# One values transfer in two pieces, and a later place for two quotients

## The chip, the cores and the metric

The kernel runs on one NeuronCore of a Trainium2 chip. The metric is the device time of one launch in microseconds. TensorE is PE (its weight loads PEld), VectorE is DVE, ScalarE is ACT, GpSimd is POOL; SyncE (SP) issues every transfer of the stages told here.

## The reference

A decoder layer over 16 batches of 112 tokens, 1024 wide, in float32, with a layer norm behind each of three parts:

```
s = silu(x @ Wg.T); in each row the half of s with the smallest |s| is set to 0
x = norm(x + (s * (x @ Wu.T)) @ Wd.T)                   # inner width 2752
q = x @ Wq (32 heads of 32); k, v = ctx @ Wk, ctx @ Wv  # 375 context rows, 8 key-value heads
x = norm(x + softmax(q k / sqrt(32)) v @ Wo)            # 4 query heads share a key-value head
x = norm(x + bf16(x) @ dequantized 4-bit weights)
```

## The kernel before

There are four passes. `context_pass` projects the context to keys and values and stores them in DRAM. `gated_query_pass` does the gated part and the queries, and stores the queries. `attend_pass` (L1292) does the attention of one batch after another, and `finish_pass` (L1660) the output projection and the last part. Each pass is a block: each engine runs its own instruction list, engines wait for each other by semaphores, and a block ends when all engines have ended theirs.

To keep float32 accuracy at a fast matmul rate, an operand is split into a high part (a rounded copy) and a low part (the rest).

In `attend_pass` a batch n has 24 steps x, three for each of the 8 key-value heads h; a step is one third (125 rows) of the 375 context rows. PE's list for a step: the transposed scores of that third (`scores`, L1616), one third of the product of the values with the exponentials of the head three heads earlier (`values`, L1635; L1629 for head 3, which isn't split), and in 16 of 24 steps a pair of score products for the next batch (`first_pair`, L1601) from which DVE takes row maxima (`maxima`, L1530). At step 18 PE turns the maxima (L1607), at step 19 ACT makes their high part (L1473), at step 20 DVE the low part (L1534), and SP writes both into the operand of the next batch (`put_max`, L149).

ACT takes the exponential of the scores (L1483), makes the high part of heads 1, 2, 4 (L1490) and copies each head's product out of PSUM (`take`, L1497); before it takes a head's product it waits, at even heads, until the store of an earlier one has landed. DVE makes the high part of heads 0, 5, 6, 7 (L1544). POOL makes all low parts (L1463) apart from head 3's; in the first eight batches it also makes one low part of the output weights each (L1451). In the last batch DVE makes the low parts of heads 2, 5 and 7 itself (`split_lo`, L1562). The buffers for the high and the low parts are three deep each.

SP's list for a batch: stacks of keys and queries for the next two batches in quarters (`fetch_qk`, four transfers each, L145), stores of the products of two heads (`put_o`, L1398 and L1400), a load of output weights in the first eight batches (L1411), and at head 7 the values of the next batch: `fetch_v`, L1387, one transfer (L1390) of 125 rows (partitions) of 6336 bytes from DRAM into one of two buffers, once the product of the batch before has been read. PE waits for the values at the first product of a batch, which is at step 9 of that batch. The values of batch 0 are loaded in the pass before (L841), at its step 26.

In the last batch SP also loads the numerators, addends and reciprocals of the first two tiles of `finish_pass` (`load_tile`, L169). `quotients(i)` (L1552) on DVE waits for those of tile i, adds (L1555) and multiplies (L1557). It stands in DVE's list at step 14 (tile 0) and at step 17 (tile 1) of the last batch. DVE's high and low parts of head h come at step 3(h + 1), those of head 7 behind the last step. ACT then makes the high part of tile 0 behind its last exponential (L1519) and POOL its low part behind its last low part of the attention (L1466). `finish_pass` starts with the high and low part of tile 1, PE with 8 idle products and the projection of tile 0.

Of the kernel before, what the change touches and what calls it, by code (L numbers as in the profile page):

```python
# [6 lines left out]
F32 = mybir.dt.float32  # L7
# [9 lines left out]
B, S, D = 16, 112, 1024  # L17
# [13 lines left out]
KN = C // KT  # L31
# [37 lines left out]
class Carry:  # L69
# [67 lines left out]
    def fetch_qk(self, sp, qd, kd, n, f):  # L137

        p, stack = n % 2, 3 * HD
        q_rows = self.qs[p][:, f].bitcast(F32).rearrange("d j m q -> d (j m q)")  # L140
        k_rows = self.ks[p][:, f].bitcast(F32).rearrange("d v c -> d (v c)")
        key = kd[n, 2 * (f % 2) + f // 2]
        for dst, src in ((q_rows[0:2 * HD], qd[n, f]), (k_rows[0:HD], key[0:HD]),
                         (q_rows[2 * HD:stack], qd[n, f, 0:HD]), (k_rows[HD:stack], key)):
            sp.dma_start(dst, src).then_inc(self.qk_loaded[p][f], 16)  # L145

    def put_max(self, eng, n, i):

# [477 lines left out]
def gated_query_pass(nc, cy, x_t, w_gu, w_d, w_d_tail, x_tok, w_q, ident_f, ident_b, y_dram, y1_dram, qd, q_v, k_v, vd):  # L626
# [28 lines left out]
    with ExitStack() as ctx:  # L655
# [95 lines left out]
        def _(sp):  # L751
# [61 lines left out]
            for n in range(XR, NALL + AHEAD + 4):  # L813
                if n < NALL:
                    load(n)
                g, c = divmod(n, N_CH)
                if c == DOWN + CC + 7 and g < G:
                    store_y(g, 0)
                if g > 0 and c == 7:
                    store_y(g - 1, 1)  # L820
                if g + 1 < G and c + 2 in X_AT:
                    load_x(g + 1, X_AT.index(c + 2))
                p = n - N - AHEAD
                for b in tokens_at(p + 2):
                    load_y(b)
                    load_tokens(b)
                for b in turn_at(p - 1):
                    store_y1(b)
                if 0 <= p - 3 < G * KD:
                    store_q(p - 3)  # L830
                if p == 20:
                    cy.await_context(sp)
                    for s in q_stored:
                        sp.wait_ge(s, 32 * KD // NQO)
                    for f in range(2):
                        cy.fetch_qk(sp, q_v, k_v, 0, f)
                if p == 23:
                    for f in range(2, NQK):
                        cy.fetch_qk(sp, q_v, k_v, 0, f)
                if p == 26:  # L840
                    sp.dma_start(cy.vs0[:].bitcast(F32).rearrange("p t v w -> p (t v w)"), vd[0]).then_inc(cy.v_loaded[0], 16)  # L841
                if p == 28:
                    for i in range(XS):
                        sp.wait_ge(y1_stored[i], 16 * len(range(i, B, XS)))
                    sp.wait_ge(back, 2 * B)
                    for f in range(2):
                        cy.fetch_qk(sp, q_v, k_v, 1, f)
                if p == 32:
                    sp.wait_ge(cy.nmh, 1)
                    cy.put_max(sp, 0, 0)  # L850
                    sp.wait_ge(cy.nml, 1)
                    cy.put_max(sp, 0, 1)
# [439 lines left out]
def attend_pass(nc, cy, kd, vd, qd, w_o, wo_hi, wo_lo, ident_f, od, rd):  # L1292
# [11 lines left out]
    PAIR_OF = {x: y for y, x in enumerate(PAIR_AT)}  # L1304
    TURN_AT = 18
    RECIP_AT = 22
    QUOTIENTS_AT = (14, 17)
    FULL = (3,)
    HI_ACT = (1, 2, 4)
    HI_DVE = tuple(h for h in range(KV) if h not in HI_ACT + FULL)  # L1310
# [11 lines left out]
    with ExitStack() as ctx:  # L1322
# [4 lines left out]
        vs = [cy.vs0, m.sb("vs1", [KN, KT, KV, VW], F32R)]  # L1327
# [12 lines left out]
        (t_scored, exped, hi_act, hi_dve, lo_pool, lo_dve, pv, o_taken, wo_hi_done, wo_lo_done) = (m.sem(n) for n in names)  # L1340
        ones, scored, maxed, nm_turned, nmh, nml, nm_put = (cy.ones, cy.scored, cy.maxed, cy.nm_turned, cy.nmh, cy.nml,
                                                            cy.nm_put)
        qk_loaded, v_loaded, o_put, recip, r_stored = cy.qk_loaded, cy.v_loaded, cy.o_put, cy.recip, cy.r_stored
        wo_loaded = [m.sem(f"wo_loaded{i}") for i in range(2)]
        block = ctx.enter_context(nc.Block())
        QK = 4 * 16
# [33 lines left out]
        @block.sync  # L1380
        def _(sp):
            def fetch_qk(n, f):
                if n >= 2:
                    sp.wait_ge(t_scored, NX * (n - 2) + NX // NQK * (f + 1))
                cy.fetch_qk(sp, qd, kd, n, f)

            def fetch_v(n):  # L1387
                if n >= 2:
                    sp.wait_ge(pv, KV * (n - 1))
                sp.dma_start(vs[n % 2][:].bitcast(F32).rearrange("p t v w -> p (t v w)"),  # L1390
                             vd[n]).then_inc(v_loaded[n % 2], 16)

            def put_o(u):

                n, h = divmod(2 * u, KV)
                row = n % GB * H + h * REP
                sp.wait_ge(o_taken, 2 * u + 2)
                sp.dma_start(od[n, h:h + 2].rearrange("h s d j q -> (s d) h (j q)"),  # L1398
                             o_ab[u % NO][0:2 * HD]).then_inc(o_put[u % NO], 16)
                sp.dma_start(den[n // GB % 2][row:row + 2 * REP, :],  # L1400
                             o_ab[u % NO][2 * HD:2 * HD + 1].rearrange("p h (j q) -> p (h j) q", q=S)
                             ).then_inc(o_put[u % NO], 16)

            def put_recip(c):
                sp.wait_ge(recip, c + 1)
                cy.put_recip(sp, rd, c)

            def load_w(k):
                if k >= 2:
                    sp.wait_ge(wo_lo_done, k - 1)  # L1410
                sp.dma_start(wo_raw[k % 2][:], w_o[:, k, :]).then_inc(wo_loaded[k % 2], 16)  # L1411

            fetch_qk(1, NQK - 2)
            cy.await_queries(sp)
            for n in range(B):
                for h in range(KV):
                    if h == 0 and n + 1 < B:
                        fetch_qk(n + 1, NQK - 1)
                    if h in (2, 4) and n + 2 < B:
                        fetch_qk(n + 2, h // 2 - 1)  # L1420
                    if h == TURN_AT // KT and n + 1 < B:
                        sp.wait_ge(nmh, n + 2)
                        cy.put_max(sp, n + 1, 0)
                        sp.wait_ge(nml, n + 2)
                        cy.put_max(sp, n + 1, 1)
                        if n + 2 < B:
                            fetch_qk(n + 2, NQK - 2)
                    if h == W_LOAD_AT and n < KV:
                        load_w(n)
                    if h == V_AT and n + 1 < B:  # L1430
                        fetch_v(n + 1)
                    if h == 2 and n == B - 1:
                        sp.wait_ge(t_scored, NX * n)
                        sp.wait_ge(r_stored, 16 * (B - GB))
                        for i in range(2):
                            load_tile(sp, od, rd, i, cy.num[i], cy.add[i], cy.rec[i], cy.o_loaded[i])
                    if (KV * n + h - LAG) % 2 == 0 and KV * n + h - LAG >= 2:
                        put_o((KV * n + h - LAG) // 2 - 1)
                    if h == RECIP_AT // KT and n % GB == 0 and n > 0:
                        put_recip(n // GB - 1)  # L1440
            for u in range((KV * B - 1 - LAG) // 2, KV * B // 2):
                put_o(u)
# [81 lines left out]
        def _(dve):  # L1524
# [27 lines left out]
            def quotients(i):  # L1552

                dve.wait_ge(cy.o_loaded[i], 16 * tile_loads(i))
                nc.vector.tensor_tensor(cy.num[i][:], cy.num[i][:], cy.add[i][:], ALU.add)  # L1555
                dve.drain()
                nc.vector.tensor_tensor(cy.num[i][:], cy.num[i][:], cy.rec[i][:], ALU.mult).then_inc(cy.normed, 1)  # L1557
# [7 lines left out]
            def follow(g):  # L1565
                if g % KV in HI_DVE:
                    split_hi(g)
                if by_dve(g):
                    split_lo(g)
# [4 lines left out]
            for n in range(B):  # L1574
                for x in range(NX):
                    h, t = divmod(x, KT)
                    for pair in pairs_at(n, x):
                        maxima(*pair)
                    if t == 0 and KV * n + h >= 1:
                        follow(KV * n + h - 1)  # L1580
                    if x == RECIP_AT and n % GB == 0 and n > 0:
                        invert(n // GB - 1)
                    if x == TURN_AT + 2 and n + 1 < B:
                        max_lo(n + 1)
                    if n == B - 1 and x in QUOTIENTS_AT:
                        quotients(QUOTIENTS_AT.index(x))
            follow(KV * B - 1)

        @block.tensor
        def _(pe):  # L1590
# [28 lines left out]
            def values(g, i):  # L1619

                n, h = divmod(g, KV)
                if i == 0:
                    if h == 0:
                        pe.wait_ge(v_loaded[n % 2], 16 * (n // 2 + 1))
                    if g >= 2:
                        pe.wait_ge(o_taken, g - 1)
                    await_hi(pe, g)
# [337 lines left out]
```

## Time and profile before

| | |
|---|---|
| median of 3 runs | 2531.68 us (2531.49 to 2536.49) |
| the profiled execution | 2542.13 us, span 2540.3 us |
| mean granted clock of PE | 0.98 |
| attention stage | about 1855 to 2308 us of the span |

Times in the rows are microseconds from the start of the span. PE is the engine with the most work. A matmul's end is modelled, so its idle time before the next can read 0.3 to 0.4 us less than the idle time of the weight loads (PEld) at the same place. The idle time before an instruction and what ended it stand in square brackets. The granted clock is a share of 2.4 GHz; 0.50 is 1.2 GHz.

### The profile page before, as it was taken

How to read it: one execution, taken by the hardware profiler on the slowest of the kernel's cores; microseconds unless marked ns; L12 is line 12 of the kernel's file. 1: busy time of each engine (PE TensorE's matmuls, PEld its weight loads, DVE VectorE, ACT ScalarE, POOL GpSimd, SP SyncE). 2: the span in 40 equal slices, each digit the busy share in tenths (PEclk: the TensorE clock that was granted, in tenths of full speed). 3: DMA queues.
4: the chain of work that ended last, by engine and by line, in shares of the span. 5: the costliest groups of instructions: out<-in, count | busy, mean ns of one | idle time of the engine just before them, and what ended most of it. 6: DMA issues, size and time to landing. Idle time of an engine off the chain costs nothing. (4 is left out here: it accounts for less than half of the span.)

```text
span 2540.3 us, 33218 instructions
## 1 busy us (share of the span) xinstructions
PE 2435.3 (96%) x12861; PEld 2126.1 (84%) x12874; DVE 1268.1 (50%) x1779; ACT 1049.1 (41%) x1531; POOL 1402.1 (55%) x626
## 2 busy tenths in 40 slices
PE   9999999999999999999999999999988888888998
PEld 9999999988999889999899998899866666656775
DVE  4762304861018820079400486254467777764665
ACT  2112235533337333363423553233266767681111
POOL 5344244865447755458554585454467887782221
PEclk9999999999999999999999999999998999998999
DMA  6565533333332343333333233589956765555772
GB/s 206 169 189 176 195 112 100 106 117 125 113 100 100 123 127 113 100 101 126 108 115 115 96 108 98 186 256 292 264 150 160 188 168 150 154 151 158 177 175 87
DMA packets 254447, 371.75 MB, mean 146 GB/s; under 512 B 126641, under 2 KB 178865, under 8 KB 254033
## 3 DMA queue, kind: packets, MB, share of 16 engines
q1 hardware_dynamic: 254288, 369.61, 49.0%
q8 instruction: 103, 1.69, 0.3%
q14 instruction: 56, 0.45, 0.1%
HBM read 290.15 MB, written 78.70 MB: 145 GB/s over the span
## 5 line engine op out<-in xcount | busy, mean ns | idle before, releaser
L995 POOL TENSOR_TENSOR gp_w_lo<-cy_raw,gp_w_hi 128x1024 fp32r<-128x1024 f32 (+2 forms) x299 | 721.0, 2413 | 611.8 <-ACT gp_w_hi L870 611.3
L183 PE MATMUL gp_acc<-gp_x_hi,gp_w_hi 128*128 128x448 f32 x1504 | 558.6, 371 | 2.6 <-ACT gp_row L921 2.5
L185 PE MATMUL gp_acc<-gp_x_hi,gp_w_lo 128*128 128x448 f32 x1504 | 550.2, 366 | 0.0
L184 PE MATMUL gp_acc<-gp_x_lo,gp_w_hi 128*128 128x448 f32 x1504 | 550.1, 366 | 0.0
L870 ACT CAST gp_w_hi<-cy_raw 128x1024 fp32r<-128x1024 f32 (+2 forms) x300 | 307.1, 1026 | 315.0 <-PE gp_acc L185 308.7
L1463 POOL TENSOR_TENSOR ap_e_lo<-ap_e,ap_e_hi 125x1344 fp32r<-125x1344 f32 x109 | 331.0, 3069 | 95.4 <-ACT ap_e_hi L1490 74.7
L183 PEld LDWEIGHTS gp_acc<-gp_x_hi,gp_w_hi 128*128 128x128 f32 x1504 | 283.2, 188 | 25.9 <-ACT gp_row L921 4.0
L185 PEld LDWEIGHTS gp_acc<-gp_x_hi,gp_w_lo 128*128 128x128 f32 x1504 | 282.9, 188 | 22.1
L184 PEld LDWEIGHTS gp_acc<-gp_x_lo,gp_w_hi 128*128 128x128 f32 x1504 | 283.3, 188 | 20.9
L481 DVE TENSOR_REDUCE gp_sel_unit<-gp_keys 112x4 f32<-112x2048 f32 x4 | 9.1, 2286 | 550.3 <-ACT gp_keys L882 550.3
L183 PE MATMUL gp_acc<-gp_h_hi,gp_w_hi 128*128 128x448 f32 (+1 forms) x704 | 267.9, 381 | 8.4 <-DVE gp_h_lo L1058 5.6
L1530 DVE TENSOR_REDUCE cy_n_max<-ap_p_s 112x2 f32<-112x750 f32 x240 | 221.5, 936 | 80.7 <-PE ap_p_s L1601 78.6
L184 PE MATMUL gp_acc<-gp_h_lo,gp_w_hi 128*128 128x448 f32 (+1 forms) x704 | 259.4, 368 | 0.0
L185 PE MATMUL gp_acc<-gp_h_hi,gp_w_lo 128*128 128x448 f32 (+1 forms) x704 | 259.3, 368 | 0.0
L1483 ACT ACTIVATE ap_e<-ap_p_t 125x448 f32<-125x448 f32 x384 | 204.6, 543 | 120.5 <-PE ap_p_t L1616 116.1
L330 POOL TENSOR_TENSOR cp_c_lo<-cp_c_raw,cp_c_hi 128x1504 fp32r<-128x1504 f32 x32 | 110.7, 3479 | 145.0 <-ACT cp_c_hi L299 145.0
L474 DVE TENSOR_SCALAR_CACHE_REDUCE gp_keep<-gp_keys,gp_sel_bound 112x2752 bf16<-112x2752 f32 (+1 forms) x56 | 158.2, 2867 | 63.9 <-ACT gp_keys L882 61.6
L1616 PE MATMUL ap_p_t<-cy_qs,cy_ks 98*125 98x448 f32 x384 | 161.5, 422 | 2.7 <-DMA cy_qs<-cy_nm_lo 1.9
L888 ACT ACTIVATE gp_act<-gp_acc 128x448 f32<-128x448 f32 x84 | 45.7, 544 | 274.4 <-PE gp_acc L185 274.4
L183 PEld LDWEIGHTS gp_acc<-gp_h_hi,gp_w_hi 128*128 128x128 f32 (+1 forms) x704 | 133.7, 190 | 23.6 <-DVE gp_h_lo L1058 6.8
L185 PEld LDWEIGHTS gp_acc<-gp_h_hi,gp_w_lo 128*128 128x128 f32 (+1 forms) x704 | 133.4, 189 | 11.6
L184 PEld LDWEIGHTS gp_acc<-gp_h_lo,gp_w_hi 128*128 128x128 f32 (+1 forms) x704 | 133.8, 190 | 9.9
(207 smaller groups left out, 4355.1 us busy)
## 6 DMA issues: line engine op xcount, KB each, us to landing
cy_raw<-in_w_gu SPq DMA_DIRECT2D x172, 512.0 KB, 3.3
cy_raw<-in_w_d SPq DMA_DIRECT2D x80, 512.0 KB, 3.6
cp_c_raw<-in_ctx_t SPq DMA_DIRECT2D x32, 750.0 KB, 6.7
cy_raw<-in_w_q SPq DMA_DIRECT2D x32, 512.0 KB, 4.6
q_scratch<-gp_q_out SPq DMA_DIRECT2D x64, 224.0 KB, 6.2
cy_qs<-q_scratch SPq DMA_DIRECT2D x64, 224.0 KB, 4.1
k_scratch<-cp_k_out SPq DMA_DIRECT2D x32, 376.0 KB
cy_ks<-k_scratch SPq DMA_DIRECT2D x64, 188.0 KB, 4.8
```

The source lines that it names most:

```text
L183: nc.tensor.matmul(out, wh, xh, start=first, stop=False)
L184: nc.tensor.matmul(out, wh, xl, start=False, stop=False)
L185: return nc.tensor.matmul(out, wl, xh, start=False, stop=last)
L330: nc.gpsimd.tensor_tensor(c_lo[p][:, ks(h), :], c_raw[p][:, ks(h), :], c_hi[p][:, ks(h), :].bitcast(F32), ALU.subtract).then_inc(lo_done, 1)
L474: self.nc.vector.tensor_scalar(self.keep[:, b, 0:width], self.keys[:, b, 0:width], bound[:, b:b + 1], None, op, ALU.add, accum_out=self.co ...
L870: last = nc.scalar.copy(o, i)
L888: nc.scalar.activation(act_t[:, c, :], a[:, 0:T], ACT.Silu).then_inc(evac, 1)
L995: last = nc.gpsimd.tensor_tensor(o, i, hi.bitcast(F32), ALU.subtract)
L1463: nc.gpsimd.tensor_tensor(e_lo[g % NLO][:], e[g % NE][:], e_hi[g % NHI][:].bitcast(F32), ALU.subtract).then_inc(lo_pool, 1)
L1483: nc.scalar.activation(e[g % NE][:, x % KT, :], p_t[x % 2][0:KN, 0:T], ACT.Exp, scale=SCALE).then_inc(exped, 1)
L1530: nc.vector.reduce_max(n_max[:, h // 2, 2 * a:2 * a + 2, h % 2], p_s[y % 2][:, :, 0:C], AX_X).then_inc(maxed, 1)
L1616: nc.tensor.matmul(p_t[x % 2][0:KN, 0:T], ks[p][0:KR, h // 2, h % 2, t * KN:(t + 1) * KN], qs[p][:, h // 2, :, h % 2, :], start=True, stop ...
```

## The change

A new method `Carry.fetch_v` issues two transfers for the values of a batch, rows 0 to 111 and rows 112 to 124, both on the same semaphore, so that the waiting value is 32 a batch in place of 16. Both places that load values call it. In the last batch of `attend_pass` the quotients of tile 0 move from step 14 to step 18, behind DVE's high and low part of head 5, and those of tile 1 from step 17 to the end of DVE's list, behind the high and low part of head 7.

```diff
+    def fetch_v(self, sp, vs, vd, n):
+
+        flat = vs[:].bitcast(F32).rearrange("p t v w -> p (t v w)")
+        for rows in (slice(0, S), slice(S, KN)):
+            sp.dma_start(flat[rows], vd[n, rows]).then_inc(self.v_loaded[n % 2], 16)
...
                 if p == 26:
-                    sp.dma_start(cy.vs0[:].bitcast(F32).rearrange("p t v w -> p (t v w)"), vd[0]).then_inc(cy.v_loaded[0], 16)
+                    cy.fetch_v(sp, cy.vs0, vd, 0)
...
-    QUOTIENTS_AT = (14, 17)
+    QUOTIENTS_AT = 18
...
             def fetch_v(n):
                 if n >= 2:
                     sp.wait_ge(pv, KV * (n - 1))
-                sp.dma_start(vs[n % 2][:].bitcast(F32).rearrange("p t v w -> p (t v w)"),
-                             vd[n]).then_inc(v_loaded[n % 2], 16)
+                cy.fetch_v(sp, vs[n % 2], vd, n)
...
-                    if n == B - 1 and x in QUOTIENTS_AT:
-                        quotients(QUOTIENTS_AT.index(x))
+                    if n == B - 1 and x == QUOTIENTS_AT:
+                        quotients(0)
             follow(KV * B - 1)
+            quotients(1)
...
-                        pe.wait_ge(v_loaded[n % 2], 16 * (n // 2 + 1))
+                        pe.wait_ge(cy.v_loaded[n % 2], 32 * (n // 2 + 1))
```

## Rows read from the trace of the kernel before

**Rows 1.** The page, busy time, share of the span and count of each engine.
```profile
PE 2435.3 (96%) x12861; PEld 2126.1 (84%) x12874; DVE 1268.1 (50%) x1779; ACT 1049.1 (41%) x1531; POOL 1402.1 (55%) x626
```

**Rows 2.** Waits from 1850 to 2300: engine, line, releaser: total us, times, longest.
```profile
PEld ap_p_o L1635 <- POOL ap_e_lo L1463: 23.8, 19, 2.3
PEld ap_p_o L1635 <- DMA cy_vs<-v_scratch: 20.1, 7, 4.5
PEld ap_p_o L1635 <- DMA ap_vs<-v_scratch: 17.9, 7, 4.2
PEld ap_p_s L1601 <- DVE cy_n_max L1530: 10.4, 10, 1.8
```

**Rows 3.** Stretches between issues of the values: length, busy times, PE clock, DMA share, GB/s.
```profile
1880.41:2104.34 223.93, 192.56 (x840) 138.43 (x839) 169.77 (x202) 158.92 (x295) 189.20 (x65) 0.93 0.65 171
2104.34:2241.93 137.59, 118.46 (x529) 85.79 (x527) 105.42 (x128) 98.26 (x181) 106.34 (x36) 0.94 0.61 157
2241.93:2266.10 24.17, 21.47 (x95) 15.50 (x94) 18.50 (x23) 17.85 (x33) 18.96 (x7) 0.93 0.42 115
```

**Rows 4.** The same view, columns PE, PEld, DVE, ACT, POOL: two single batches.
```profile
1996.32:2021.11 24.79, 22.41 (x107) 16.06 (x106) 21.73 (x27) 19.74 (x38) 23.73 (x9) 1.00 0.74 197
2129.37:2159.55 30.18, 24.47 (x104) 17.64 (x103) 21.33 (x27) 19.41 (x36) 21.73 (x8) 0.89 0.57 145
```

**Rows 5.** PE's timeline: start, us, line, tiles; one pair of products a step.
```profile
2144.47 0.83 PE L1601 MATMUL ap_p_s<-cy_ks,cy_qs 96*112 96x376 f32 x2
2146.22 0.83 PE L1601 MATMUL ap_p_s<-cy_ks,cy_qs 96*112 96x376 f32 x2
2147.68 0.51 PE L1601 MATMUL ap_p_s<-cy_ks,cy_qs 96*112 96x376 f32 x2
2148.63 0.51 PE L1601 MATMUL ap_p_s<-cy_ks,cy_qs 96*112 96x376 f32 x2
```

**Rows 6.** Timeline: two issues of the values on SP, and PE's first use of each.
```profile
1996.32 0.48 SPq L1390 DMA_DIRECT2D ap_vs<-v_scratch  x1
2006.47 0.20 PEld L1635 LDWEIGHTS ap_p_o<-ap_e_hi,ap_vs 125*66 125x66 f32 x2 [0.79 <-DMA ap_vs<-v_scratch]
2129.37 0.48 SPq L1390 DMA_DIRECT2D cy_vs<-v_scratch  x1
2141.92 1.01 PE L1635 MATMUL ap_p_o<-ap_e_hi,cy_vs 125*66 125x448 f32 x2 [4.15 <-DMA cy_vs<-v_scratch]
```

**Rows 7.** Stretches of 1 us; the values issued at 2159.55 let PE go at 2171.52.
```profile
2168.00:2169.00 1.00, 0.00 (x0) 0.00 (x0) 0.00 (x0) 1.00 (x2) 1.00 (x1) 1.00 1.00 241
2172.00:2173.00 1.00, 1.00 (x5) 0.93 (x4) 0.00 (x0) 0.00 (x0) 1.00 (x1) 0.50 0.33 97
```

**Rows 8.** The page, DMA issues: count, KB each, median us to landing.
```profile
cp_c_raw<-in_ctx_t SPq DMA_DIRECT2D x32, 750.0 KB, 6.7
ap_wo_raw<-in_w_o SPq DMA_DIRECT2D x8, 512.0 KB, 10.1
```

**Rows 9.** Timeline of the last batch's end, all engines.
```profile
2283.62 0.98 ACT L1483 ACTIVATE ap_e<-ap_p_t 125x448 f32<-125x448 f32 x2
2291.93 1.23 DVE L1555 TENSOR_TENSOR cy_num<-cy_num,cy_add 128x1024 f32<-128x1024 f32 x1 [3.56 <-DMA cy_rec<-r_scratch]
2292.78 0.53 ACT L1497 COPY ap_o_ab<-ap_p_o 66x448 f32<-66x448 f32 x1 [2.92 <-DMA cy_den<-ap_o_ab]
2294.37 1.55 DVE L1544 TENSOR_SCALAR_CACHE_REDUCE ap_e_hi<-ap_e 125x1344 fp32r<-125x1344 f32 x1
2296.07 1.35 PE L1635 MATMUL ap_p_o<-ap_e_hi,ap_vs 125*66 125x448 f32 x3 [7.55 <-DVE ap_e_hi L1544]
2300.74 2.78 DVE L1562 TENSOR_TENSOR ap_e_lo<-ap_e,ap_e_hi 125x1344 fp32r<-125x1344 f32 x1
2307.01 0.68 SPq L1400 DMA_DIRECT2D cy_den<-cy_o_ab  x1
2308.43 0.10 POOL L1739 MEMSET fp_neg_half<- 128x1 f32 x1 [2.69 <-POOLq L1322]
```

More of the change, by code:

```diff
@@ L1342, in attend_pass @@
                                                             cy.nm_put)
-        qk_loaded, v_loaded, o_put, recip, r_stored = cy.qk_loaded, cy.v_loaded, cy.o_put, cy.recip, cy.r_stored
+        qk_loaded, o_put, recip, r_stored = cy.qk_loaded, cy.o_put, cy.recip, cy.r_stored
         wo_loaded = [m.sem(f"wo_loaded{i}") for i in range(2)]
```

## The prediction

> **What bounds the kernel now.** I read the page's busy shares first, then the waits of the attention stage, then that stage by stretches, and last single instructions. PE is busy in 96% of the span [rows 1]; most of the kernel is a PE stream, and only holes in it can be won. Of the weight loads' waits in the attention stage (about 1855 to 2308 us), the longest by cause are those of the value products for the values transfer: 20.1 + 17.9 = 38.0 us in 14 times, one for each batch from the second to the fifteenth. Behind them come POOL's low parts (23.8 us) and DVE's maxima (10.4 us) [rows 2]. The 0.1 us by which such a wait overstates the loss is left in.
>
> The stretches are cut at the issues of the values transfer: eight of them in 223.93 us, five in 137.59, the last in 24.17; clocks 0.93, 0.94, 0.93 [rows 3]. The two stretches of rows 4 show what a wait costs: 24.79 us at clock 1.00 where PE waited 0.79, 30.18 us at 0.89 where it waited some 4.5. So a long wait is paid twice. Behind it PE runs at half clock (1.2 of 2.4 GHz) for a few microseconds: one step of the loop takes 1.75 us (2144.47 to 2146.22), a step at full clock 0.95 [rows 5].
>
> The transfer is slow. Issued at 2129.37, it let PE go at 2141.92, 12.55 us later; the quickest took 10.15 us (1996.32 to 2006.47) [rows 6]. The mean of the fourteen is 11.7. PE would have been ready 8.2 us after the issue (2137.6; its wait is read from the same row) and 9.4 us after it in the other. Why slow: early in the transfer all DMA engines are busy (share 1.00, 241 GB/s), but at its end and just behind it the share stays at 0.33 with 97 GB/s [rows 7]. That is 5 engines of 16 (0.31). Five engines carry its 125 rows, and what was queued behind it on those five still runs while eleven rest.
>
> **The split of the transfer.** It now goes as 112 rows and 13 rows. What does it take? From below: on five engines each carries 773.4 / 5 = 155 KB in 11.7 us; 693 KB on sixteen is 43 KB each, at the same pace 3.3 us, with the second issue (0.48 us later, the issue's own length in rows 6) 3.8 us. From above: the 512 KB rows of the output weights, 128 partitions wide and in this same stage, land after 10.1 us [rows 8]; by size that is 15.3 us for 773.4 KB, and it is the far end. The nearest row in size and width is the context's 750 KB in 6.7 us [rows 8]: 6.9 us by size, 7.4 with the second issue. I take 7.4. The weights' row is the worse guide, because it is issued behind four stacks of keys and queries and its own share of the five clogged engines comes last. 7.4 is under the 8.2 to 9.4 us that PE leaves, with only 0.8 us to spare in the tightest.
>
> What goes, by groups of stretches. Waits: 19.5 us in the eight, 16.2 in the five, 2.25 in the last (together the 38.0 of rows 2). Half clock: at most (1 - clock) x length, 15.7, 8.3 and 1.7 us [rows 3]; part of that time passed in waiting, and some dips may have another cause, so I take three quarters: 11.8, 6.2, 1.3. New lengths:
> - the eight: 223.93 - 19.5 - 11.8 = 192.6 us. POOL is the next limit: it worked 189.20 us in them [rows 3], seven low parts a batch and the weights' in addition. They can't be shorter than 189.2. In the 24.79 us stretch POOL was busy 23.73 us [rows 4], so this limit has been touched already.
> - the five: 137.59 - 16.2 - 6.2 = 115.2 us; POOL's work there is 106.34, DVE's 105.42 [rows 3], both below.
> - the last: 24.17 - 2.25 - 1.3 = 20.6 us, over POOL's 18.96.
> Sum 328.4 against 385.69: 57.3 us less. What is late next is then POOL's low part in the first half, and in the second DVE's maxima by a little.
>
> The extra issue costs SP 0.48 us in each of 15 batches. Behind it in SP's queue stand two output transfers and the last quarter of the next keys and queries, needed some 15 steps later; they now find no clogged engines. The row maxima are issued ahead of it. I cost it at nothing; without that cover it is 0.48 x 15 = 7 us. The transfer for the first batch, issued in the stage before, has tens of microseconds.
>
> **The closing batch.** DVE makes the next pass's quotients before head 5's high part and waits for their data: until 2291.93, 3.56 us; the high part comes only at 2294.37, PE waits 7.55 us for it until 2296.07 [rows 9]. Now head 5's scores, exponentiated at about 2284.1 (first of the pair at 2283.62), are split at once. Step by step, with a high part of DVE at 1.55 us, a pass of quotients at 1.23 and a low part at 2.78 where POOL works beside it [rows 9], without POOL like a high part, 1.6: high 5 to 2285.8, low 5 to 2287.4, first quotients (two passes and a gap) to 2289.9, high 6 to 2291.5, high 7 to 2293.1, low 7 to 2295.9. POOL's low 6 runs from 2291.5 to 2294.6 (106.34 us for some 35 of them in rows 3, 3.0 each). PE: head 5 by 2290.5; head 6 not before ACT has taken head 4's outputs, which waits for a store and ended at 2293.31 [rows 9], so 2293.3 to 2295.9; head 7 to 2298.2 at half clock. ACT takes it by 2298.8, SP's last two stores are issued by 2300.2 (before: 0.59 + 0.67 us, the last at 2307.01), and the next pass opens 0.7 us behind: 2300.9 against 2308.43 [rows 9], 7.5 us less. DVE's second quotients, now last, end near 2299.6 to 2300.9 if POOL slows them and lie beside this. Bounds: nothing, if the end of the pass waits for them and for their data; 9.4 us, if all of PE's waits go. The pass behind is PE-bound and moves forward whole.
>
> **Sum.** 57.3 + 7.5 = 64.8 us. The profiled execution took 2542.13 us (span 2540.3), 10.4 above the median of 2531.68. 2542.13 - 64.8 = 2477.3; by the ratio of the two, 2467 us.
>
> **Rivals.**
> 1. The next limits bite earlier. The waits gave POOL and DVE time to catch up; that goes. For it: POOL already holds PE 23.8 us. Against: rows 4, where 24.79 us passed with hardly a wait. Price: the eight at 24.8 us (198.3), the five at 24.2 (121), the last 22.2, the closing batch 5: 44 + 5 = 49 us less, 2483.
> 2. The transfer is hidden only in part. It lands near 10.2 us, today's quickest, because DMA is busy on all engines when it starts [rows 7]. PE then waits 1 to 2 us a batch, 17 to 20 us, without the dips: about 46 us less, 2486.
> 3. The split brings nothing: the bytes, not the engines, set the pace. 241 GB/s at full share speaks for it, the 0.33 at the end against. Only the closing batch remains, less up to 7 us of issues: 2531.7 - 7.5 + 7 = 2531. (The Trainium skill, page "DMA: Bandwidth & Descriptors", section "Rules for kernel authors": two transfers to disjoint partitions are not worth it, since both use the same engines; use one 128-partition transfer. It presupposes halves that each spread over all 16, and the share of 0.33 in rows 7 says that the one transfer of today doesn't. By the rule the time would be this rival's 2531, by the row the forecast.)
> 4. Slower. The values on all 16 engines queue behind the keys and queries everywhere, as the output weights do, and land after 15.3 us. Each of 14 waits grows by 15.3 - 11.7 = 3.6 us: 50 us, less 7.5: 2574. It decides once the mean landing is over 11.7 + 7.5 / 14 = 12.2 us. For it stands the 10.1 of rows 8; against it, that no transfer would then find idle engines, and eleven are idle in rows 7.
>
> **How the numbers follow.** Forecast 0.64, rivals 0.14, 0.12, 0.06 and 0.04. The forecast's own range is 2456 to 2476: all of the half-clock losses and 9.4 us at one end (the eight at POOL's 189.2: 34.7 + 24.5 + 4.0 + 9.4 = 72.6 us, 2459), a closing batch without gain at the other (57.3 us, 2475), and 1 to 3 us on each side for the runs' own spread. With the first two rivals the range is 2456 to 2492. About 0.2%, 5 us, can be told from no change. Faster: the forecast and rivals 1 and 2, 0.9 and a little; same: rival 3; slower: rival 4.
>
> **What the profile would show.** Right: no wait of the value products for values in the waits of the attention stage, or under 3 us in all; clocks of 0.98 and more by stretch; stretches of about 24.1 us in the first half and 23.0 in the second; the DMA share no longer lingering at 0.33; the wait of 7.55 us gone, and one of 2 to 3 us for ACT's taking of head 4 in its place. Wrong: waits for the values that remain at 1 us and more (rival 2), more than 35 us of waits for POOL and over 20 for DVE's maxima (rival 1), or row maxima that arrive later, which would put the extra issue or the fuller engines on the path.

## The result and the profile after

The changed kernel takes 2477.14 us (2475.1 to 2481.15, 4 runs) against 2533.91 us (4 runs) of the kernel before: ratio 0.9778, 95% interval 0.976 to 0.9796. The forecast was 2467 us with a range of 2456 to 2492. Run again twice, the changed kernel had ratios of 0.9776 and 0.9767. By the medians the gain is 56.8 us, and 64.7 were forecast; the time lies 1 us outside the forecast's own range (2456 to 2476), in the part that the range has by rivals 1 and 2.

The profiled execution took 2481.15 us (span 2479.3), 61.0 us under the one of before; the forecast's sum was 64.8. Where the 61.0 us came from, cut at the first and last issue of the values transfer and at the opening of the next pass, as in [rows 3, 9]:

| part | before | after | less | forecast |
|---|---|---|---|---|
| up to the first such issue of the attention | 1880.41 | 1877.33 | 3.1 | 0 |
| first eight stretches | 223.93 | 198.89 | 25.0 | 31.3 |
| next five | 137.59 | 116.26 | 21.3 | 22.4 |
| last | 24.17 | 20.58 | 3.6 | 3.6 |
| from the last issue to the next pass | 42.33 | 34.66 | 7.7 | 7.5 |
| the next pass | 231.87 | 231.58 | 0.3 | 0 |

The first row is no part of the change: in the kernels told below this moment lay between 1870.7 and 1879.9 us, whatever was changed behind it.

The waits of the attention stage after, 1850 to 2260 us (engine, line, releaser: total us, times, longest):
```profile
PEld ap_p_o L1641 <- POOL ap_e_lo L1468: 33.8, 37, 2.3
PEld ap_p_s L1607 <- DVE cy_n_max L1535: 11.2, 10, 1.8
PEld ap_p_o L1641 <- ACT ap_o_ab L1502: 4.5, 8, 3.0
PEld ap_p_o L1641 <- DMA cy_vs<-v_scratch: 0.8, 1, 0.8
PE ap_p_o L1641 <- POOL ap_e_lo L1468: 18.2, 12, 1.9
```
Of 38.0 us of waits for the values in 14 times one of 0.8 us is left [rows 2]. The weight loads' waits for POOL have grown from 23.8 to 33.8 us, and from 19 to 37 times. The last line is PE's own idle time for the same cause, and that has hardly grown. Before, the view had:
```profile
PE ap_p_o L1635 <- DMA cy_vs<-v_scratch: 17.7, 7, 4.2
PE ap_p_o L1635 <- POOL ap_e_lo L1463: 16.2, 11, 1.9
PE ap_p_o L1635 <- DMA ap_vs<-v_scratch: 15.6, 7, 3.8
```
So the two engine rows of one wait differ: 38.0 us by the weight loads is 33.3 us by PE.

The stretches after (ends, length, busy PE, PEld, DVE, ACT, POOL, clock, DMA share, GB/s), first by group, then four single batches of the first eight and one of the five:
```profile
1877.33:2076.22 198.89, 183.89 (x840) 129.66 (x839) 169.53 (x202) 157.61 (x295) 189.85 (x65) 0.98 0.71 192
2076.22:2192.48 116.26, 111.01 (x529) 81.10 (x527) 105.27 (x128) 97.12 (x181) 106.75 (x36) 1.00 0.69 186
2192.48:2213.06 20.58, 19.74 (x95) 14.35 (x94) 18.49 (x23) 17.52 (x33) 19.04 (x7) 1.00 0.51 136
...
1902.02:1926.68 24.66, 22.77 (x107) 15.88 (x106) 21.11 (x26) 19.78 (x38) 23.71 (x9) 1.00 0.71 196
1926.68:1952.08 25.40, 23.51 (x107) 17.33 (x106) 21.12 (x26) 19.94 (x38) 23.76 (x9) 0.93 0.70 191
1952.08:1976.78 24.70, 22.80 (x107) 15.88 (x106) 21.13 (x26) 19.77 (x38) 23.73 (x9) 1.00 0.75 196
2001.44:2026.88 25.44, 23.53 (x105) 17.09 (x104) 21.14 (x26) 19.73 (x37) 23.72 (x9) 0.93 0.70 192
2122.61:2145.46 22.85, 21.99 (x107) 16.20 (x106) 20.77 (x26) 19.32 (x37) 21.30 (x8) 1.00 0.71 189
```
The clock is 1.00 where it was 0.94 [rows 3], apart from two batches of the first eight at 0.93, which are 0.75 us longer than their neighbours. The DMA share rose from 0.65 and 0.61 to 0.71 and 0.69: the same bytes in less time. It no longer lingers near 5/16: of the slices of 1 us between the first and the last issue of the values, 48 of 385 had a share of 0.30 to 0.36 before, and 9 of 335 have it now.

One batch's waits of PE for POOL after, from PEld's timeline:
```profile
1906.94 0.13 PEld L1641 LDWEIGHTS ap_p_o<-ap_e_lo,ap_vs 125*66 125x66 f32 x1 [2.26 <-POOL ap_e_lo L1468]
1909.97 0.13 PEld L1641 LDWEIGHTS ap_p_o<-ap_e_lo,ap_vs 125*66 125x66 f32 x1 [0.37 <-POOL ap_e_lo L1468]
1913.01 0.13 PEld L1641 LDWEIGHTS ap_p_o<-ap_e_lo,cy_vs 125*66 125x66 f32 x1 [0.49 <-POOL ap_e_lo L1468]
1916.06 0.13 PEld L1641 LDWEIGHTS ap_p_o<-ap_e_lo,cy_vs 125*66 125x66 f32 x1 [0.38 <-POOL ap_e_lo L1468]
1919.11 0.14 PEld L1641 LDWEIGHTS ap_p_o<-ap_e_lo,cy_vs 125*66 125x66 f32 x1 [0.39 <-POOL ap_e_lo L1468]
```
After the wait of 2.3 us PE walks at POOL's pace, one head in 3.05 us, for four heads more. Before, such a row held the first wait and the 0.36; then the values' wait came and POOL had caught up.

The end of the last batch after, answering to [rows 9]:
```profile
2238.95 0.96 ACT L1502 COPY ap_o_ab<-ap_p_o 66x448 f32<-66x448 f32 x2 [1.08 <-DMA cy_den<-ap_o_ab]
2239.53 0.72 PE L1641 MATMUL ap_p_o<-ap_e_hi,ap_vs 125*66 125x448 f32 x2 [2.60 <-ACT ap_o_ab L1502]
2241.35 3.68 POOL L1471 TENSOR_TENSOR cy_o_lo<-cy_num,cy_o_hi 128x1024 fp32r<-128x1024 f32 x1
2241.44 1.38 PE L1641 MATMUL ap_p_o<-ap_e_lo,ap_vs 125*66 125x448 f32 x3 [0.81 <-POOL ap_e_lo L1468]
2242.72 3.38 DVE L1560 TENSOR_TENSOR cy_num<-cy_num,cy_add 128x1024 f32<-128x1024 f32 x1
2246.18 1.23 DVE L1562 TENSOR_TENSOR cy_num<-cy_num,cy_rec 128x1024 f32<-128x1024 f32 x1
2246.30 0.67 SPq L1405 DMA_DIRECT2D cy_den<-cy_o_ab  x1
2247.72 0.10 POOL L1745 MEMSET fp_neg_half<- 128x1 f32 x1 [2.69 <-POOLq L1328]
```
The wait of 7.55 us for DVE is gone; 2.60 us for ACT's taking of head 4 stands in its place, as forecast. DVE's last quotients end at 2247.41, 0.44 us behind SP's last store (issue over at 2246.97). The next pass opens 0.75 us behind that issue, as it did before (0.74 us, where DVE had nothing late); so the store explains the opening, and the quotients end beside it. The trace doesn't show which of the two is the last.

### The profile page after: what moved, and what is told of

Read it like the earlier page. It is cut to its first block and busy times, and to the rows that moved or that the text cites. A ratio compares the mean times of both kernels' runs of the same rounds, so it can differ in the third digit from the quotient of the medians.

```text
span 2479.3 us, 33234 instructions
## 1 busy us (share of the span) xinstructions
PE 2412.9 (97%) x12861; PEld 2108.1 (85%) x12874; DVE 1269.1 (51%) x1779; ACT 1046.4 (42%) x1531; POOL 1403.4 (57%) x626
## 5 line engine op out<-in xcount | busy, mean ns | idle before, releaser
L1468 POOL TENSOR_TENSOR ap_e_lo<-ap_e,ap_e_hi 125x1344 fp32r<-125x1344 f32 x109 | 332.1, 3083 | 36.6 <-ACT ap_e_hi L1495 23.8
L189 PEld LDWEIGHTS gp_acc<-gp_h_hi,gp_w_hi 128*128 128x128 f32 (+1 forms) x704 | 133.1, 189 | 23.5 <-DVE gp_h_lo L1064 6.8
L191 PEld LDWEIGHTS gp_acc<-gp_h_hi,gp_w_lo 128*128 128x128 f32 (+1 forms) x704 | 132.9, 189 | 11.8
```

The lines of the kernel that those rows point to most:

```text
L189: nc.tensor.matmul(out, wh, xh, start=first, stop=False)
L191: return nc.tensor.matmul(out, wl, xh, start=False, stop=last)
L1468: nc.gpsimd.tensor_tensor(e_lo[g % NLO][:], e[g % NE][:], e_hi[g % NHI][:].bitcast(F32), ALU.subtract).then_inc(lo_pool, 1)
```

## The experiments

### The split alone

```diff
-    QUOTIENTS_AT = 18            # changed kernel
+    QUOTIENTS_AT = (14, 17)      # and both quotients back there
```


> The changed kernel with the quotients back at steps 14 and 17. Theory (two independent gains): the stretches between the issues of the values are as in the changed kernel, 198.9 + 116.3 + 20.6 us (together 335.7 against 385.7 before), and the end of the last batch is as before, from the last issue of the values to the next pass 42.3 us against 34.7 in the changed kernel. Time about 53 us under the kernel before, ratio 0.979 to 0.980. Rival (the closing batch only looked faster because it started without a backlog): the end takes under 38 us even with the quotients at their old steps, and the time equals the changed kernel's.

Measured: 2487.79 us, ratio 0.9789 (0.9764 to 0.9814). The stretches:
```profile
1879.85:2081.53 201.68, 186.42 (x839) 133.94 (x838) 169.59 (x202) 157.77 (x295) 189.80 (x65) 0.96 0.69 189
2081.53:2197.27 115.74, 111.03 (x529) 81.34 (x528) 105.28 (x128) 97.10 (x181) 106.74 (x36) 1.00 0.69 187
2197.27:2217.94 20.67, 19.85 (x95) 14.33 (x94) 18.51 (x23) 17.60 (x33) 19.02 (x7) 1.00 0.49 134
```
Together 338.1 us against 385.7 of before, and 41.5 us from the last issue to the next pass. The stretches' gain belongs to the split alone, the end's to the quotients. The stretches show this and the ratios don't: the intervals of this kernel and of the changed one overlap. The rival falls, since the end took 41.5 us and not under 38. The 2.4 us over the forecast 335.7 are half-clock dips: five batches of the first eight ran 25.4 us or longer at a clock of 0.93 here, two in the changed kernel's first profile.

### The quotients alone

```diff
-    QUOTIENTS_AT = (14, 17)      # kernel before
+    QUOTIENTS_AT = 18            # and quotients(1) behind follow(KV * B - 1)
```


> The kernel before with the quotients at step 18 and at the end of DVE's list; values in one transfer of 125 rows. Theory: 7.7 us less, all behind the last issue of the values (34.7 us from there to the next pass instead of 42.3), ratio about 0.997; the fourteen waits for the values stay at 38 us. Rival: the end is limited by something that the split brought, and the ratio is 1.000.

Measured: 2525.55 us, ratio 0.9952 (0.9934 to 0.9969). The end took 34.6 us, and the waits for the values were still 34.7 us:
```profile
PEld ap_p_o L1636 <- POOL ap_e_lo L1463: 23.5, 15, 2.3
PEld ap_p_o L1636 <- DMA cy_vs<-v_scratch: 18.4, 7, 3.9
PEld ap_p_o L1636 <- DMA ap_vs<-v_scratch: 16.3, 8, 4.3
```
The ratio says 12 us, the place of the change 7.7; the interval's upper end, 0.9969, is 7.9 us. The stretches were 6 us shorter than before without a reason in the edit (one profiled execution each), so the end's length is the better measure.

### The cut at row 115

```diff
-        for rows in (slice(0, S), slice(S, KN)):
+        for rows in (slice(0, 115), slice(115, KN)):
```


> The changed kernel with the values cut at row 115 in place of row 112: again two transfers with nearly the same sizes, but 115 = 5 x 23. Theory (what matters is over how many DMA engines the long piece goes, 5 here as for 125 rows): each of the five engines has 23 rows in place of 25, so that the landing takes about 11 us and the waits for the values come back, 28 to 36 us in all, with half clock behind them; the DMA share lingers at 0.33; ratio to the kernel before 0.985 to 0.995. Rival (two pieces in flight, or a smaller first one, are what helps): as the changed kernel, ratio 0.978, hardly a wait for values.

Measured: 2528.05 us, ratio 0.9941 (0.9912 to 0.997). Waits and stretches:
```profile
PEld ap_p_o L1641 <- DMA cy_vs<-v_scratch: 20.6, 7, 4.4
PEld ap_p_o L1641 <- DMA ap_vs<-v_scratch: 17.5, 7, 5.3
```
```profile
1879.29:2103.48 224.19, 194.01 (x840) 140.60 (x839) 169.54 (x202) 159.65 (x295) 189.28 (x65) 0.92 0.66 170
2103.48:2244.36 140.88, 120.38 (x529) 87.13 (x528) 105.47 (x128) 98.42 (x181) 106.31 (x36) 0.93 0.60 154
```
Two signs of the five engines are back as well: a DMA share of 0.32 (the last number but one of the first line) in the slice at whose end one batch's values landed, issued at 2160.34, and the output weights' landing, here and then in the changed kernel (DMA issues from 1850 to 2300: count, KB, median us to landing):
```profile
2172.00:2173.00 1.00, 0.00 (x0) 0.00 (x0) 0.00 (x0) 0.00 (x0) 1.00 (x1) 0.50 0.32 92
ap_wo_raw<-in_w_o SPq DMA_DIRECT2D x8, 512.0 KB, 9.9
ap_wo_raw<-in_w_o SPq DMA_DIRECT2D x8, 512.0 KB, 5.4
```
All of the split's gain is gone: 38.1 us of waits and clocks of 0.92 and 0.93, as before. Over the 13 waits ahead of the last batch the values landed 12.0 us behind their issue (before, over its 14: 11.7). Two pieces bring nothing by themselves, nor does a first piece shorter by 8%; three rows decide. 125 and 115 both divide by 5, and both leave a share near 5/16; 112 divides by 16 and leaves hardly any. The output weights land after 10.1 us with 125 rows [rows 8], 9.9 with 115 and 5.4 with 112: it was the values' five engines that held them up. I had expected somewhat shorter waits (28 to 36 us). The Trainium skill, "DMA: Bandwidth & Descriptors", section "Why a DMA increments its semaphore by 16 and not by 1", says that a transfer uses the largest number of engines up to 16 that divides its slowest dimension. By that rule it is 16 for 112 rows, 5 for 125 and for 115. The traces agree: a DMA share of 0.33 behind the 125 rows [rows 7], of 0.32 behind the 115, and 115 rows as slow as 125.

### The values issued late

```diff
                     if h == 0 and n + 1 < B:
                         fetch_qk(n + 1, NQK - 1)
+                    if h == 0 and n > 0:
+                        fetch_v(n)
-                    if h == V_AT and n + 1 < B:
-                        fetch_v(n + 1)
```


> The changed kernel with the values' issue moved behind the last quarter of the keys and queries, about 4 us later, so that PE waits for them in every batch and the time from issue to landing can be read. It settles the 7.4 us of the prediction, which the changed kernel's trace can't show where nothing waits. Expected: landing 6.5 to 8.5 us behind the issue (forecast 7.4), so waits of 2 to 4 us in each of 15 batches and a time some 40 us over the changed kernel's. If the landing is over 9 us, the changed kernel is hidden only by an earlier issue's luck; at 4 us, the pace per engine of the old transfer (13 KB a us) was the better guide than the context's 6.7 us.

Measured: 2517.85 us (one run). PE waited for the values in 12 batches, 31.0 us. The longest and the shortest landing:
```profile
2148.28 1.02 SPq L151 DMA_DIRECT2D ap_vs<-v_scratch  x2
2157.09 0.30 PEld L1641 LDWEIGHTS ap_p_o<-ap_e_hi,ap_vs 125*66 125x66 f32 x2 [5.41 <-DMA ap_vs<-v_scratch]
...
2207.79 1.02 SPq L151 DMA_DIRECT2D ap_vs<-v_scratch  x2
2213.32 0.30 PEld L1641 LDWEIGHTS ap_p_o<-ap_e_hi,ap_vs 125*66 125x66 f32 x2 [3.59 <-DMA ap_vs<-v_scratch]
```
8.81 and 5.53 us; the mean of the 12 is 7.1 us, where 6.5 to 8.5 had been expected, and the waits were 0.5 to 5.4 us in 12 batches, not 2 to 4 in 15. The batches without a wait can't be read; they landed in time. The forecast's 7.4 holds as a mean, and the spread explains the changed kernel's one wait: its values landed 8.84 us behind their issue (2145.46 to 2154.30), and PE was ready after 8.0.

### Four pieces

```diff
-        for rows in (slice(0, S), slice(S, KN)):
+        for rows in (slice(0, 48), slice(48, 96), slice(96, S), slice(S, KN)):
```


> The changed kernel with the values in four transfers (48, 48, 16 and 13 rows), each but the last over 16 engines. It prices the extra issue that the prediction put at nothing: SP gets two more, some 1 us a batch. Theory (SP has room and nothing behind it in its queue is late): stretches within 0.2 us a batch of the changed kernel's, ratio 0.978, waits for the values under 3 us in all. Rival (an issue of 0.5 us goes to the path): 15 to 16 us more, ratio 0.984. The landing of the last piece moves by 1 us, so a few waits of under 1 us may appear.

Measured: 2479.24 us, ratio 0.977 (0.9744 to 0.9797). Stretches 200.70, 115.66 and 20.59 us, end 34.65, and no wait for the values at all. SP's issues take 1.95 us a batch in place of 1.02. The rival's 15 us aren't there: the first eight are 1.8 us longer than the changed kernel's 198.89, with four batches at a clock of 0.93 where that had two, and the other stretches aren't longer. The extra issues cost nothing that can be seen.

### The weights' low part at head 4

```diff
-    W_LOAD_AT, W_SPLIT_AT = 3, 6
+    W_LOAD_AT, W_SPLIT_AT = 3, 4
...
-                    if x == KT * W_SPLIT_AT + 2 and n < KV:
+                    if x == KT * W_SPLIT_AT - 1 and n < KV:
```
(SP loads the weights one batch earlier, those of batch 0 at its start.)

> The changed kernel with the output weights' low part on POOL ahead of head 4's low part instead of behind head 5's, ACT's high part of them at step 11 instead of 20, and their load a batch earlier. It looks at why the first eight stretches took 198.9 us and not the 192.6 forecast. Theory (the place of that piece of work: it stands in the middle of POOL's unbroken row, PE waits 2.3 us for the next low part in each of eight batches, while POOL idles 0.8 us at head 4 of the next one): the stretches fall from 24.7 to about 23.9 us, PE's waits for POOL from 33.8 us to under 20, 5 to 7 us less than the changed kernel, ratio 0.9755. Rival (POOL's total work of 23.7 us a batch sets the pace, wherever the piece stands): the stretches stay at 24.7 and the waits only move to another head.

Measured: 2467.98 us, ratio 0.9717 (0.9689 to 0.9744). The first eight stretches as one, and the waits for POOL:
```profile
1876.29:2067.02 190.73, 185.02 (x840) 125.41 (x839) 167.35 (x202) 158.39 (x295) 188.83 (x65) 1.00 0.72 197
```
```profile
PEld ap_p_o L1643 <- POOL ap_e_lo L1470: 31.9, 59, 1.4
```
PE's own idle time for POOL within the first eight stretches, in the changed kernel and here:
```profile
PE ap_p_o L1641 <- POOL ap_e_lo L1468: 14.5, 8, 1.9
PE ap_p_o L1643 <- POOL ap_e_lo L1470: 4.6, 16, 0.3
```
The stretches of the first half fall to 23.9 us (the first 23.5), 8 us less in all, with no dip of the clock. POOL is busy for 188.83 of 190.73 us, 99%: now its amount is the limit; in the changed kernel it was the order of the work (POOL busy for 95%). The edit moved three things, POOL's piece, ACT's high part and the load, and no run parts them. The weight loads' waits for POOL hardly fell in sum (31.9 us; I had expected under 20), and I had read that sum as lost time. It isn't: PE's own idle time fell by 9.9 us, and the stretches by 8.2. The wait of 2.3 us a batch is gone, and the small waits of the weight loads that stand in its place mostly pass while PE still multiplies. In a second profile of the changed kernel that sum is 27.9 us, less than the 33.8 of the first, though its first eight stretches are 3.6 us longer.

Again, beside the changed kernel, five runs of each:

> The changed kernel, as the measure for the next one on the same chip: ratio 0.978, first eight stretches 199 to 203 us by the number of half-clock dips behind the 2.3 us waits for POOL.

> The kernel with the weights' low part at head 4 once more, now beside the changed kernel on one chip. Theory (place, not amount, of POOL's work): first eight stretches 190.7 us at clock 1.00 with no wait for POOL over 1.4 us, 8 to 12 us less than the changed kernel, ratio 0.973 or lower, and the two intervals apart. Rival (the first run of it was a lucky chip): ratio within 0.002 of the changed kernel's.

Changed kernel 2480.47 us (2477.73 to 2482.93), ratio 0.9767 (0.9742 to 0.9791); this one 2470.13 us (2467.69 to 2472.59), ratio 0.9732 (0.9708 to 0.9756). First eight stretches 198.85 and 190.80 us. The intervals of the ratios overlap by 0.0014, against what was expected; the runs themselves, five each, don't overlap, and the difference is 10.3 us. This version beats both kernels.

### The end reordered

```diff
-    QUOTIENTS_AT = 18
+    QUOTIENTS_AT = 21
...
+                    if h == 5 and n == B - 1:       # tile 1's load, out of h == 2
+                        load_tile(sp, od, rd, 1, cy.num[1], cy.add[1], cy.rec[1], cy.o_loaded[1])
...
+            take(KV * B - LAG - 1)                   # ACT, ahead of tile 0's high part
             act.wait_ge(cy.normed, 1)
```
(With the weights' low part at head 4; `quotients(1)` moved to the head of DVE's list in `finish_pass`.)

> The changed kernel as it is, beside the next two on one chip. Expected: ratio 0.978 again, stretches of 198.9, 116.3 and 20.6 us, 34.7 us at the end; 2 of the first eight batches may again be 0.75 us longer at clock 0.93.

> The kernel with the weights' low part at head 4, and in the last batch: SP issues the load of tile 1 only behind the store of the pair before, ACT takes head 4's product ahead of tile 0's high part, DVE makes tile 0's quotients behind head 6's high part, and tile 1's in the next pass. Theory (in the changed kernel PE waits 2.6 us for ACT's taking of head 4, which waits for a store that SP issued late, and DVE's last quotients end the pass at the same time as SP's last store): the end takes 33 to 33.6 us in place of 34.6, which only the trace can tell; ratio some 0.971. Rival: the quotients beside POOL's low part of head 6 slow DVE so far that the end stays at 34.6.

Measured: the changed kernel 2481.55 us, ratio 0.9776 (0.9753 to 0.9798), with stretches of 202.52, 115.67 and 20.59 us; in six of its first eight batches the clock dipped. The reordered one 2471.18 us, ratio 0.9739 (0.9713 to 0.9765), and its end took 36.9 us, 2.2 longer, not 1 to 1.6 shorter. DVE, POOL and PE there, from the timeline:
```profile
2224.99 1.22 DVE L1564 TENSOR_TENSOR cy_num<-cy_num,cy_add 128x1024 f32<-128x1024 f32 x1
2225.15 3.95 POOL L1471 TENSOR_TENSOR ap_e_lo<-ap_e,ap_e_hi 125x1344 fp32r<-125x1344 f32 x1 [2.96 <-DVE ap_e_hi L1553]
2226.28 3.90 DVE L1566 TENSOR_TENSOR cy_num<-cy_num,cy_rec 128x1024 f32<-128x1024 f32 x1
2235.16 1.38 PE L1644 MATMUL ap_p_o<-ap_e_lo,ap_vs 125*66 125x448 f32 x3 [2.07 <-DVE ap_e_lo L1571]
```
The rival's mechanism holds, and it costs more than the rival said: a pass of quotients beside POOL's low part of head 6 takes 3.90 us in place of 1.23, and head 7's parts come late. ACT, which makes tile 0's high part ahead of taking head 5's product, waits 4.70 us for these quotients, and PE's high part of head 7 waits for ACT. Step 18 is a better place: POOL is idle from 2232.95 to 2238.34 in the changed kernel, and both passes of the quotients lie in it (2234.28 to 2236.80). What the later load of tile 1 and the earlier taking of head 4 are worth by themselves isn't shown.

## Why the prediction was right, and where its sum was off

- **The bound.** Right: PE's holes by the values' transfer were the largest that this edit could close, and 38.0 us of waits became 0.8.
- **Five engines.** Right, and shown by the cut at row 115, which has two transfers and none of the gain. So rival 3 falls, and the rule against splitting in two doesn't apply to a transfer that uses 5 engines of 16. One reading beside it was off: the slice with all engines busy in [rows 7] lies 8.5 us behind the issue, so it isn't early in the transfer. The share stays at 0.6 and more until 2170; it falls to 0.44 and 0.34 only in the last 1.5 us before the landing, and stays near 0.33 for some 4 us behind it.
- **The landing of 7.4 us.** 7.1 on average by the late issue. The context's row was the right guide. The output weights' 10.1 us was not, for the reason given: in the changed kernel they land after 5.4 us. So rival 4 falls. Rival 2 shows in one batch of 15, by 0.8 us. The room was a little smaller than read: the row gives PE ready at 2137.77 by its own wait (4.15) or 2137.4 by the weight load's, 8.4 or 8.0 us behind the issue, not 2137.6 and 8.2.
- **A wait is paid twice.** The clock rose to 1.00 in all six later stretches at once with the waits' end. But not every long wait was paid twice before: the first one, 3.06 us by the weight loads, left its stretch (1880.41 to 1907.46) at 1.00.
- **The waits' size.** They were read from the weight loads, 38.0 us, and the overstatement was put at 0.1 us a wait. By PE's own idle time they are 33.3 us, 0.3 less each. The term was up to 4.7 us too large: 2.4 in the first eight stretches (17.1 in place of 19.5) and 1.9 in the five (14.3 in place of 16.2).
- **The first eight stretches.** This is the term that was mis-sized most: 192.6 forecast, 198.89 measured, and up to 202.5 in other executions. The step took POOL's total (189.2 us) for its limit and subtracted the values' waits and the half clock without anything in exchange. By PE's columns the missing 6.3 us are the 2.4 above, 0.7 of other idle time, and 3.1 of busy time, which fell by 8.7 us and not by 11.8; the two batches still at 0.93 are 1.5 of these. Behind the wait of 2.3 us PE goes at POOL's pace, 3.05 us a head for four heads more, where the values' wait used to let POOL catch up. A head of the second half takes 2.86 (22.85 us for eight); that makes 0.8 us a batch, by estimate. Rival 1, which said that POOL would lose its time to catch up and priced it at 198.3 us, was right for these eight, and wrong for the five, which it put at 121. Moving the weights' piece, which leaves the amount as it is, gave 190.73: under the forecast.
- **The five and the last.** 116.26 us for a forecast of 115.2, and 20.58 for 20.6. In part this is luck: the busy time fell by 7.5 us where three quarters of the half-clock time had been taken (6.2), and that made up for most of the waits' overstatement.
- **Half clock that stayed.** The forecast removed the dips with the values' waits. In the first eight batches a wait of 2.3 us for POOL sometimes brings one: in two, six and two of eight in three profiles of the changed kernel, in five with the split alone and in four with four pieces. With the weights' piece moved, where no such wait in the first eight is over 0.7 us, there was none.
- **The extra issue at nothing.** Right, by the four pieces.
- **The closing batch.** 7.7 us for 7.5. Each of its steps came within 0.3 us of the forecast when counted from the last issue of the values, but for PE, which ended head 5 by 0.5 us and began head 6 by 0.7 us earlier. PE's list went as forecast, with the wait for ACT. The second quotients were put at 2299.6 to 2300.9 and beside the end; they ended there, 2300.45 in these times, though the add took 3.38 us: it had to wait for POOL.

So the time fell inside the stated range for the reason forecast, less a part that rival 1 had named. Of the range's far side nothing came: no row maxima were later (1.5 us of waits for them in three times, before 3.8), and DVE's maxima (11.2 us) stayed under rival 1's sign of 20, POOL's waits (33.8) just under its 35.

## What to carry to other kernels

Where PE waits for a transfer whose partitions aren't a multiple of 16, try cutting it so that the large piece's are, even if the rest must go as a small second one; a DMA share near 5/16 at the transfer's end and behind it was the sign here. When the largest wait of a stage is closed, look at which engine used it to catch up, and at the order of that engine's work as much as at its amount. Price a wait by PE's own idle time and by the length of the stretch; a sum of the weight loads' waits is no gain to be had.

## What the runs showed of the hardware

- 115 partitions are as slow as 125 (12.0 and 11.7 us to landing), 112 plus 13 take 7.1 us (read with the issue 4 us later). Transfers issued after them are held up too: the output weights' 512 KB land after 10.1 us (125), 9.9 (115) and 5.4 (112).
- A DVE pass with two inputs that starts while a POOL pass runs ends as if it had begun about when POOL's was over. An add or multiply over 128 x 1024 takes 1.21 us alone; it took 2.45, 3.38 and 3.90 us beside POOL in three traces and each time ended 1.07 or 1.08 us behind POOL's pass. The same holds the other way round: POOL's pass over 128 x 1024 takes 2.36 us when it starts first and 3.68 behind DVE's low part of head 7, in the kernel before as in the changed one. DVE's high part, with one input, takes 1.55 us with and without POOL.
- PE's clock fell to its half level in some batches behind idle times of 2.3 us and in others not: some 25.4 to 25.7 us a batch with it, some 24.7 without, by the same program. What decides it, no run here shows.
